# The context of cross-attention: turned by VectorE instead of TensorE, for all batches but the first

## The reference

```python
a = _layer_norm(audio_kv, ln_gamma, ln_beta)              # 16 x 375 x 512
Q = (hidden_states @ Wq.T).reshape(B, Tt, HEADS, HEAD_DIM).transpose(0, 2, 1, 3)
K = (a @ Wk.T).reshape(B, Ta, HEADS, HEAD_DIM).transpose(0, 2, 1, 3)
V = (a @ Wv.T).reshape(B, Ta, HEADS, HEAD_DIM).transpose(0, 2, 1, 3)
scores = jnp.einsum('bhtd,bhsd->bhts', Q, K) * scale       # 16 heads of 32
scores = jnp.where(mask, scores, jnp.float32(-jnp.inf))
attn = jax.nn.softmax(scores, axis=-1)
out = jnp.einsum('bhts,bhsd->bhtd', attn, V)
return hidden_states + jnp.tanh(gate) * (out @ Wo.T)
```

## Time and profile before

| | |
|---|---|
| median of 3 runs | 1399.43 us (1397.38 to 1405.21) |
| the profiled execution: its own time | 1399.84 us |
| the profiled execution: span, first to last instruction | 1398.0 us |
| mean granted TensorE clock over the span | 0.979 |
| TensorE busy | 1319.0 us (94% of the span) |
| VectorE, ScalarE, GpSimd busy | 939.5, 752.2, 528.5 us |

### The profile page before, as it was taken

How to read it: one execution, slowest core, us unless ns; L and a number is a source line. 1 busy time by engine, 2 the same in 40 slices (tenths; PEclk the granted TensorE clock), 3 DMA queues, 4 the chain that set the end, 5 groups by cost and what they waited for, 6 DMA issues and landing times.

```text
span 1398.0 us, 42906 instructions
## 1 busy us (share of the span) xinstructions
PE 1319.0 (94%) x17120; PEld 936.5 (67%) x17120; DVE 939.5 (67%) x2416; ACT 752.2 (54%) x1804; POOL 528.5 (38%) x582
## 2 busy tenths in 40 slices
PE   6999999999999999897899999999999999999967
PEld 5777777777777777666666666766676666667624
DVE  3555555555555555547578888888888789887852
ACT  4776677676676677532434453445444544454342
POOL 2221112222222222113547545654566355644550
PEclk9999999999999999987899999999999999999978
DMA  7333322222222222213000010010100010000000
GB/s 228 100 105 107 98 63 69 75 71 70 65 76 76 76 69 92 63 50 136 15 14 22 22 28 14 23 27 21 24 14 26 21 28 11 25 21 21 8 15 14
DMA packets 39402, 73.48 MB, mean 53 GB/s; under 512 B 17781, under 2 KB 20469, under 8 KB 37701
## 3 DMA queue, kind: packets, MB, share of 16 engines
q1 hardware_dynamic: 39237, 71.01, 17.2%
HBM read 60.01 MB, written 7.57 MB: 48 GB/s over the span
## 4 chain that ended last, share of the span: by engine, by line
PE 73%; DVE 13%; issue 8%; ACT 2%; DMA 2%; POOL 1%; SPq 1%; DVEq 0%; POOLq 0%; ACTq 0%
PE b_bank L2017 15%; PE b_bank L2023 12%; PE ring_bank L703 7%; PE ring_bank L704 6%; PE ring_bank L705 6%; PE av_bank L789 4%; PE score_banks L762 4%; DVE probs L450 3%; PE b_bank L2132 3%; PE score_banks L749 3%; PE b_bank L2158 2%; DVE bv L1404 2%; DVE probsT L467 2%; PE av_bank L775 2%; DVE ktil L1398 1%
## 5 line engine op out<-in xcount | busy, mean ns | idle before, releaser
L1139 POOL TENSOR_TENSOR rst<-rp,st 128x448 f32<-128x448 f32 x192 | 202.5, 1078 | 34.9 <-DVE st L1425 32.0
L450 DVE CUSTOM_DVE_ANT_0 probs<-score_banks,unmask 112x375 f32<-112x375 f32 x256 | 124.9, 545 | 93.0 <-issue 93.0
L595 ACT ACTIVATE probs<-probs,least_inv 112x375 f32<-112x375 f32 x256 | 152.7, 609 | 32.5 <-DVE least_inv L450 32.5
L467 DVE SCALAR_TENSOR_TENSOR probsT<-score_banks,least_cols 125x448 f32<-125x448 f32 x192 | 108.0, 618 | 54.2 <-PE score_banks L762 51.8
L610 ACT ACTIVATE probsT<-probsT,key_mask 125x448 f32<-125x448 f32 x192 | 114.7, 662 | 47.6 <-DVE probsT L467 47.4
L1131 POOL TENSOR_TENSOR xm<-mixed,xa 128x448 f32<-128x448 f32 x80 | 89.6, 1129 | 96.1 <-DVE mixed L1354 90.7
L375 POOL TENSOR_TENSOR ctx_rstd<-ctx_var_eps,a_eps_exp 125x3 f32<-125x3 f32 x16 | 13.9, 866 | 272.7 <-DVE ctx_var_eps L423 272.7
L340 POOL TENSOR_TENSOR aT_lo<-whole,aT_hi 128x375 fp32r<-128x375 f32 x64 | 59.0, 922 | 152.3 <-ACT whole L576 150.2
L703 PE MATMUL ring_bank<-aT_hi,wk_lo 128*128 128x376 f32 x256 | 91.2, 356 | 0.9 <-issue 0.9
L1159 POOL TENSOR_TENSOR cen_r<-wkv,sq_r 128x448 fp32r<-128x448 f32 x15 | 17.1, 1140 | 196.6 <-ACT sq_r L1829 196.6
L1354 DVE SCALAR_TENSOR_TENSOR mixed<-b_bank,vec_sb,sx 128x112 f32<-128x112 f32 x320 | 82.5, 324 | 5.6 <-POOL xm L1131 3.9
(11 more groups left out here) (197 smaller groups left out, 3156.6 us busy)
## 6 DMA issues: line engine op xcount, KB each, us to landing
least_cols<-values_of_two_batches SPq DMA_DIRECT2D x32, 437.5 KB
ctx_tok<-in_ctx SPq DMA_DIRECT2D x16, 672.0 KB
xT_sb<-in_xT SPq DMA_DIRECT2D x16, 224.0 KB, 3.0
inv_cols<-values_of_two_batches SPq DMA_DIRECT2D x128, 28.0 KB, 3.7
x_tok<-in_x SPq DMA_DIRECT2D x16, 224.0 KB, 2.7
x_between_layers<-x_tok SPq DMA_DIRECT2D x16, 224.0 KB, 4.6
b_x<-x_between_layers SPq DMA_DIRECT2D x16, 224.0 KB, 2.6
out_dram<-ln_tok SPq DMA_DIRECT2D x16, 224.0 KB, 2.3
```

The lines of the kernel that those rows point to most:

```text
L450: dve.tensor_tensor_reduce(out=probs[:, g % 2, i], in0=score_bank[0:T, i, 0:TC], in1=unmask[:, m[1]], scale=-SCALE, scalar=-LOWEST, op0=AL ...
L467: dve.scalar_tensor_tensor(out=probsT[:, g % 2, k].rearrange("p (i t) -> p i t", t=T), in0=score_bank[0:TK, :, k * T:(k + 1) * T], scalar= ...
L595: act.activation(probs[:, g % 2, i], probs[:, g % 2, i], ACT.Exp, scale=-1.0, bias=least_at(m, g, i), accum_out=sums[:, g, i:i + 1]).then_ ...
L1139: pool.tensor_tensor(by_chunk(rst[:, j % NPROD]), by_chunk(rp[:].rearrange("p c t -> p (c t)")), state_of(j), ALU.mult).then_inc(s_pprod, 1)
```

## The change

From batch 1 on TensorE no longer transposes the context. The context is loaded a second time in blocks of 32 tokens by 32 channels (`ctx_quads`: four quarters of the partitions hold four blocks of 128 channels), VectorE turns the blocks of 32 by 32 (`turn_ctx`, four instructions), GpSimd subtracts the means (`centre_ctx`), VectorE multiplies with the inverse deviations (`scale_ctx`), ScalarE applies gamma and beta in place (`affine_aT`) and rounds to `aT_hi` (`copy_aT`). Means and inverse deviations now lie along the free dimension, so they go to DRAM and come back on all 128 partitions (`spread_stats`). The first batch goes the old way. The channels are in another order over partitions, so `wk`, `wv`, gamma and beta are loaded in pieces; tokens are in plain order, so the two masks are read plainly (`key_mask8`). `least_cols` comes in two transfers, 112 and 13 partitions. Queries are projected in three calls, one of which stands where three of four turned chunks stood.

```diff
 
-RING = ["K0", "S1", "K1", "K2", "K3", "V0", "V1", "V2", "S0", "T0", "T1", "T2", "T3", "qa", "qb"]
-RING_START = ["T0", "T1", "T2", "T3", "qa", "qb"]
+RING = ["K0", "S1", "K1", "K2", "K3", "V0", "V1", "V2", "S0", "qa", "qb", "qc"]
+RING_START = ["T0", "T1", "T2", "T3", "qa", "qb", "qc"]
+QUERY = {"qa": (0, 1), "qb": (1, 2), "qc": (2, 4)}
 RING_FIRST = [u for u in RING if u != "S1"]
-RING_NEXT_LAST = [u for u in RING if u[0] not in "Tq"]
+RING_NEXT_LAST = [u for u in RING if u[0] != "q"]
...
+    def load_quads(sp, b):
+
+        if at_least(b, 2):
+            sp.wait_ge(s_turned, count(later(b, -2), 1, 1))
+        else:
+            sp.wait_ge(s_ring, unit_done((-1, 1), f"T{C - 1}"))
+        tokens = A["ctx"][index(b)]
+        for q in range(QUADS):
+            channels, rows = slice(q * P, (q + 1) * P), q * BLOCK
+            sp.dma_start(ctx_quads[rows:rows + BLOCK, 0:TB - 1],
+                             tokens[0:TC - TAIL, channels].rearrange("(k r) d -> r k d", r=BLOCK)).then_inc(s_quads, 16)
+            sp.dma_start(ctx_quads[rows:rows + TAIL, TB - 1], tokens[TC - TAIL:TC, channels]).then_inc(s_quads, 16)
...
+            if is_batch(b, 1):
+                sp.wait_ge(s_ctxn, 2)
+            elif at_least(b, 1):
+                sp.wait_ge(s_stats, count(later(b, -1), 2, 1))
...
+        def spread_stats(b):
+            sp.wait_ge(s_rstd, count(b, 1, 1))
+            sp.dma_start(stats_in_dram(b).rearrange("a (p k) -> p a k", k=KT), meanvar[:]).then_inc(s_stat_out, 16)
+            sp.wait_ge(s_stat_out, count(later(b, -1), 16, 16))
+            sp.dma_start(stat_rows[:], stats_in_dram(b).rearrange("(o a) t -> o a t", o=1).broadcast_to([P, 2, TC])).then_inc(s_stat_in, 16)
...
-            sp.dma_start(least_cols[:, 2 * half:2 * half + 2],
-                         rows_in_dram(half, 0).rearrange("(o g) f -> o g f", o=1).broadcast_to([TK, 2, HG * T])).then_inc(s_least_in[half], 16)
+            for part in CTX_PARTS:
+                sp.dma_start(least_cols[part, 2 * half:2 * half + 2],
+                             rows_in_dram(half, 0).rearrange("(o g) f -> o g f", o=1).broadcast_to(
+                                 [part.stop - part.start, 2, HG * T])).then_inc(s_least_in[half], 16)
...
+        def load_turned(name):
+            for q in range(QUADS):
+                sp.dma_start(W[name][q * BLOCK:(q + 1) * BLOCK], A[name][:, q].rearrange("(c j) d -> j c d", j=BLOCK)).then_inc(s_w[name], 16)
...
+        for q in range(QUADS):
+            for i, name in enumerate(("ln_gamma", "ln_beta")):
+                sp.dma_start(affine_ctx[q * BLOCK:(q + 1) * BLOCK, i], A["vec"][:, VEC[name], q].rearrange("(c j) -> j c", j=BLOCK),
+                             allow_slow_non_contiguous=True).then_inc(s_w["vec"], 16)
+        sp.wait_ge(s_ctx, 32)
         load_x((0, 0))
         sp.dma_start(wq[:], A["wq"]).then_inc(s_w["wq"], 16)
-        sp.dma_start(W["wk"][:], A["wk"]).then_inc(s_w["wk"], 16)
+        load_turned("wk")
         sp.dma_start(mask8[:], A["mask"].rearrange("(o b) t -> o b t", o=1).broadcast_to([T, B, TC])).then_inc(s_w["mask"], 16)
-        sp.dma_start(W["wv"][:], A["wv"]).then_inc(s_w["wv"], 16)
+        load_turned("wv")
         load_ctx((0, 1))
         load_x((0, 1))
         sp.dma_start(gate[:], A["gate"].broadcast_to([T, 1])).then_inc(s_w["gate"], 16)
-        sp.dma_start(key_mask8[:], A["mask"].rearrange("b (p k) -> p b k", p=TK),
+        sp.dma_start(key_mask8[:], A["mask"].rearrange("b (k p) -> p b k", p=TK),
                      allow_slow_non_contiguous=True).then_inc(s_w["key_mask"], 16)
-        sp.dma_start(wo[:], A["wo"]).then_inc(s_w["wo"], 16)
+        load_quads(sp, (0, 1))
...
             if normalise and not is_batch(n, B - 2):
                 load_x(later(n, 2))
+            if normalise:
+                spread_stats(later(n, 1))
+            if is_batch(n, 0):
+                sp.dma_start(wo[:], A["wo"]).then_inc(s_w["wo"], 16)
...
             if normalise and not is_batch(n, B - 2):
                 load_ctx(later(n, 2))
+                load_quads(sp, later(n, 2))
...
+        def centre_ctx(b):
+            pool.wait_ge(s_stat_in, count(later(b, -1), 16, 16))
+            pool.wait_ge(s_turned, count(later(b, -1), 1, 1))
+            for h in range(2):
+                part = ctxT[:, 2 * h:2 * h + 2, 0:TC]
+                pool.tensor_tensor(part, part, stat_rows[:, 0:1].broadcast_to([P, 2, TC]), ALU.subtract).then_inc(s_cent, 1)
...
+        def turn_ctx(b):
+            dve.wait_ge(s_quads, count(later(b, -1), 32 * QUADS, 32 * QUADS))
+            dve.wait_ge(s_split, count(later(b, -1), C, C))
+            for c in range(C):
+                last = dve.transpose(ctxT[:, c].rearrange("p (k r) -> p k r", r=BLOCK), ctx_quads[:, :, c * BLOCK:(c + 1) * BLOCK])
+            last.then_inc(s_turned, 1)
+
+        def scale_ctx(b):
+            for h in range(2):
+                dve.wait_ge(s_cent, count(later(b, -1), 2, h + 1))
+                part = ctxT[:, 2 * h:2 * h + 2, 0:TC]
+                dve.tensor_tensor(part, part, stat_rows[:, 1:2].broadcast_to([P, 2, TC]), ALU.mult).then_inc(s_ctxn, 1)
...
                 return last_step(m, l)
             if finish:
                 scale_attn(l, 1)
+            if normalise:
+                ln_stats(later(n, 1))
             if attend:
                 invert_sums(m, 1)
             if finish:
                 residual(l)
             if attend:
                 shift_scores(m, 0)
+            if normalise:
+                turn_ctx(later(n, 1))
...
             if project:
                 mask_scores(n, 0, range(HG))
             if is_batch(n, 0):
@@ -523,13 +601,11 @@
             if attend:
                 shift_scores(m, 1)
             if normalise:
-                ln_stats(later(n, 1))
+                scale_ctx(later(n, 1))
             if is_batch(n, B - 1):
                 second.stats1((0, 0))
             if project:
                 mask_scores(n, 1, range(HG))
-            if normalise:
-                ln_apply(later(n, 1))
             if is_batch(n, B - 1):
...
+        def affine_aT(b, c):
+            act.wait_ge(s_ctxn, count(b, 2, c // 2 + 1))
+            act.activation(ctxT[:, c, 0:TC], ctxT[:, c, 0:TC], ACT.Identity, scale=affine_ctx[:, 0, c:c + 1],
+                           bias=affine_ctx[:, 1, c:c + 1]).then_inc(s_whole, 1)
...
+            if normalise:
+                for c in range(C):
+                    affine_aT(p, c)
             if attend:
                 exps_key_major(m, 2)
             if project:
@@ -659,26 +748,28 @@
...
             if project:
                 copy_rows(n, 0)
             if normalise:
-                for c in range(3):
+                for c in range(C):
                     copy_aT(p, c)
+                copy_query(p, "a")
             if attend:
                 exps_key_major(m, 3)
             if is_batch(n, B - 1):
                 second.xa_affine((0, 0))
             if normalise:
-                copy_aT(p, 3)
-                copy_query(p, "a", slice(0, 2))
+                copy_query(p, "b")
             if project:
                 exps(n, 2, range(HG))
                 exps(n, 3, range(HG))
             if normalise:
-                copy_query(p, "b", slice(2, 4))
...
@@ -849,8 +943,7 @@
                 scores(n, 2)
                 turn_rows(n, 0)
             if normalise:
-                for c in range(3):
-                    transpose_ctx(p, c)
+                project_query(p, "a")
             if attend:
                 weigh_values(m, 2)
                 key_major_scores(m, 3)
@@ -858,20 +951,19 @@
                 pe.wait_ge(s_ringev, unit_done(n, "V2"))
                 second.transpose_x((0, 0))
             if normalise:
-                transpose_ctx(p, 3)
-                project_query(p, "a", (0, 1))
+                project_query(p, "b")
             if project:
                 scores(n, 3)
             if attend:
                 weigh_values(m, 3)
             if normalise:
-                project_query(p, "b", (2, 3))
-
-        pe.wait_ge(s_w["ident"], 16)
+                project_query(p, "c")
```

154 lines of the change are left out of this document (88 added, 66 removed).

## The result

| | before | changed |
|---|---|---|
| median | 1400.49 us, 4 runs (1397.38 to 1405.21) | 1413.26 us, 4 runs (1412.03 to 1418.06) |
| ratio, 95% interval | | 1.0103 (1.008 to 1.0126) |
| span of the profiled execution | 1398.0 us | 1410.2 us |

What follows compares the result with a forecast made beforehand. TensorE, busy 94%, was taken as full, with a second chain through VectorE and back behind it. 1399.8 + 12.1 + 1.8 + 0.7 - 2.3 - 1.5 - 1.4 = 1409.2 us, range 1395 to 1419.

Steps and rivals of the forecast that it cites:

- main term: Start, SyncE's queue: 6,000 mask runs delay `ctx_quads`, so VectorE's first maxima and V0 come late; +12.1 us, bounds +6.7 and +20.
- first maxima and V0 late: Start: first maxima at 38.1 us instead of 25.96, held by `ctx_quads` behind the mask, V0 moving with them; +12.1 us.
- the clock after the stand: Start: TensorE, after standing 12 us between K3 and V0, runs at half clock for a while; +1.8 us.
- `wv_lo` beside `centre_ctx`: Step 0: VectorE's and GpSimd's work come at the same time and slow four instructions; +0.7 us, between 0 and 1.4.
- transposes out, step 0: Step 0: `scores(0, 2)` to `scores(0, 3)` shrinks from 5.52 to 3.2 us; -2.3 us, bounds -2.3 and 0.
- transposes out, 14 steps: Steps 1 to 14: only the second chain link shortens, 3.00 to 2.89 us; 14 x 0.11 = -1.5 us, bounds 0 and -21.
- `least_cols` in two parts: Step 16: landing 1.5 us sooner removes VectorE's wait of 1.47 us; -1.4 us, bounds -1.5 and 0.
- The term of the steps: Step 5: TensorE waits 0.5 to 0.7 us before `key_major_scores(m, 3)`, about 1.2 before `scores(n, 3)`; step 0.1 us shorter.
- rival C: Start: it costs more, with mask runs at twice the price; 1417 us, 8%.
- Rival A: Steps: the 1.5 us of transposes come back in full each step, the chain having room; 1389.7 us, 12%.
- Zeros: Steps: VectorE's, GpSimd's and ScalarE's new work and SyncE's queue there cost 0 us.
- Rival D: Every step: `scale_ctx` waits for `centre_ctx` because the means land late; one us a step gives 1423 us, 10%.

Runs made afterwards that it cites:

- weights_whole: The changed kernel with `wk` and `wv` loaded in one transfer each, in runs of 8,192 bytes instead of 2,048; 1410.75 us, ratio 1.0083 to the kernel before.
- mask_bytes: The kernel before with `key_mask8` read in 6,000 runs of one byte instead of 2,000 of three; 1400.61 us, ratio 1.0005.
- fill: The changed kernel with `project_value(n, 2)`'s last chunk behind `scores(n, 2)` and query unit a behind `key_major_scores(m, 3)`; 1403.29 us, ratio 1.0028 to the kernel before.
- fill_before: The kernel before with only `project_value(n, 2)`'s last channel chunk moved behind `scores(n, 2)`; 1402.14 us, ratio 1.0024.
- least_parts: The kernel before with `least_cols` sent in two parts of 112 and 13 partitions, nothing else; 1398.13 us, ratio 0.9991.
- start_free: The changed kernel with `key_mask` sent behind `wo` and step 0's old VectorE and ScalarE order, except `ln_stats` ahead of the maxima; 1411.02 us, ratio 1.0078.
- mask_late: The changed kernel with `key_mask` sent behind `wo` in step 0 instead of ahead of `ctx_quads`; 1412.37 us, ratio 1.0102 to the kernel before.
- own_queue: The changed kernel with `key_mask` sent from ScalarE's queue and, in step 0, the kernel before's order on VectorE and ScalarE; 1410.7 us, ratio 1.0084.
- mask_act: The changed kernel with `key_mask` sent from ScalarE's queue, ahead of all ScalarE does, instead of SyncE's; 1413.32 us, ratio 1.0101 to the kernel before.
- two_parts: The changed kernel with 750 mask runs ahead, 5,250 from ScalarE's queue at step 0's end, and step 0's old VectorE and ScalarE order; 1410.37 us, ratio 1.0075.

## Why the prediction was right, point by point

I said 1409 us, 1395 to 1419, slower with 63%. It is 1413.26, by the mechanism that I had named. But the main term was too small by 9.4 us, two gains were larger than I had them (by 1.9 and 0.9 us), and one gain of 3.9 us was not foreseen.

| step of the sum | predicted | measured | shown by |
|---|---|---|---|
| first maxima and V0 late | +12.1 | +21.5 | timelines |
| the clock after the stand | +1.8 | +2.45 | V0 to the second `scores`: 5.42 less 2.97 |
| `wv_lo` beside `centre_ctx` | +0.7 | 0 | they did not meet: 2.49 us as before |
| transposes out, step 0 | -2.3 | -2.2 | 23.96 to 21.74 |
| transposes out, 14 steps | -1.5 | -2.4 | 21.70 to 19.27 |
| `least_cols` in two parts | -1.4 | -3.3 | 19.27 to 16.0 |
| start of the second layer | none | -3.9 | 16.0 to 12.1 |
| sum on 1399.84 | 1409.2 | 1412.0 | |

The measured terms are differences along one timeline, so that they add up shows nothing by itself. That 1413 lies in my forecast's own band of 1405 to 1414 is partly luck: with the losses of the first three rows as measured and all gains as I had them, the sum would have been 1418.6, at the upper edge of the range.

**The main term** failed in four places. I let the mask's runs begin at 23.2 us as before; they began at 27.1, 3.9 later, because `wk` and `wv` now come in pieces with runs of 2,048 bytes (weights_whole gives 3.8 of it back). I had missed that edit's price. The runs took 10.8 us instead of 8.1 (mask_bytes): between my middle and rival C's price, which was twice. SyncE was therefore free at 37.3, not 30.7, after an issue of 22.5 us where I had said 16. And `ctx_quads` landed 8.2 us after that, not 5.5: I had counted its issues and a latency, but not that its own 1,500 runs of 512 bytes follow one another for 7 us. Turning took 1.96 us against my 1.84.

**The term of the steps** was right in kind. Waits of 0.34 and 1.05 us stand where I had put 0.5 to 0.7 and 1.2, and the links are 3.06 and 2.90. Rival A (the transposes' time comes back) fell, and fill shows why: without the transposes the chain sets the time, and starting it 0.7 us sooner shortens each step by as much. fill_before agrees for the other side, with half of the edit: with the transposes TensorE is full and no order of this kind helps. What the removal freed is room, and the unchanged order of TensorE left it empty.

**Zeros.** VectorE's, GpSimd's and ScalarE's new work in the steps cost nothing, as said: a step is 0.17 us shorter, not longer. Rival D fell: `scale_ctx` waited for `centre_ctx` 5.2 us in all, in two places.

**Step 16** gave more than its wait of 1.47 us because behind the shorter stand the granted clock was 1.00 and not 0.50. The Trainium skill, DMA: Bandwidth & Descriptors, was of two minds; the traces (a wait of 0.82 us instead of 2.39, in least_parts too) agree with "Why a DMA increments its semaphore by 16 and not by 1", and not with "Rules for kernel authors", as far as that one wait goes.

**The second layer's gain** I can only read, not claim to have tested. The kernel before, then the changed kernel (SyncE and TensorE):

```profile
623.64 0.33 SPq L262 DMA_DIRECT2D x_between_layers<-x_tok  x1
627.08 0.35 SPq L1086 DMA_DIRECT2D b_wo<-in_b_wo  x1
...
645.29 3.99 PE L2158 MATMUL b_bank<-vbd,kz 64*32 64x128 f32 x128 [2.32 <-DMA vbd<-vtok]
```

```profile
639.66 0.33 SPq L299 DMA_DIRECT2D x_between_layers<-x_tok  x1
641.92 0.35 SPq L1178 DMA_DIRECT2D b_wo<-in_b_wo  x1
...
658.89 3.21 PE L2250 MATMUL b_bank<-vbd,kz 64*32 64x128 f32 x128
```

The store takes 3.44 us until SyncE goes on, and 2.26 in the changed kernel; behind it stand the weights, and behind them `vbd`. Of the 3.9 us the wait for `vbd` is 2.3, and 0.8 is that the 128 matmuls behind it take 3.21 us instead of 3.99; the rest comes by 680 us and I did not trace it. In the kernel before three packets of the two queues of instructions, one of 16 KB and two of 8 KB, fall into the store (its transfers from 623.6 to 627.1 us, by queue: packets, MB, share of the engines):

```profile
q8 instruction: 1, 0.02, 2.6%
q14 instruction: 2, 0.02, 1.2%
```

In the changed kernel none does; the packet of 16 KB comes 4.8 us behind the store's issue. This holds in every trace: 0.6 to 0.7 us behind the issue, with one or two of 8 KB, in the four kernels with transposes, and 3.2 us or more in the ten without. All three kernels that I made from the one before take 3.3 to 3.5 us there and wait 1.9 to 2.7 us for `vbd`; all nine made from the changed one take 2.3 and wait at most 0.3. So this part belongs to the program, not to chance. That it is these packets, or which of them, was not tried by itself.

## What to carry to other kernels

Count runs, not bytes: a table of 6 KB in 6,000 runs cost 7 to 8 us more than in 2,000, the largest single part of what the start lost, and wherever I put it, it delayed something that was soon needed. If work is taken off a full engine and its time doesn't come back, look for the chain that now shows as short waits, and move other work into them; in the steps the removal alone was worth 2.4 us, half of the reordering alone nothing, removal and reordering together 12. Putting the wait for a first load behind what the next engine already waits for brought V0 forward by 5 and 8 us (start_free against mask_late, own_queue against mask_act) but the time by no more than 3, since the next link took over: the whole path, the rows of the load itself included, has to be added up.

## What the hardware showed that I had not expected

Two engines at once. GpSimd's passes of 750 elements took 1.80 us, and VectorE's `scale_ctx` of the same size 0.93 us, but 2.51 once:

```profile
L506 DVE TENSOR_TENSOR ctxT<-ctxT,ctx_stat_rows x30: 926/932/2507, 54.7 to 555.0; 128x750 f32<-128x750 f32 x30
```

The long one began at 54.73 us, while GpSimd's second pass ran until 56.44; the 1.58 us over are nearly that overlap of 1.71. In start_free `wv_lo` came beside GpSimd's mask work and took 4.01 us instead of 2.49. The Trainium skill, SBUF — State Buffer, "Who interferes with whom", has the two exclude each other for a whole instruction; these rows agree, and my +0.7 for such a meeting would have been too low by half (4.01 less 2.49 is 1.5).

The price of a run. On SyncE's queue 6,000 runs took 10.8 to 11.9 us in the six kernels that have them there in one piece, while the DMA engines show a share of 0.56. The Trainium skill, DMA: Bandwidth & Descriptors, "Why a DMA increments its semaphore by 16 and not by 1", gives a transfer whose slowest dimension is 125 five engines of the sixteen. The row does not bear that out by itself: five engines busy without a break are a share of 0.31. By that rule parts of 112 and 13 partitions would shorten the mask, as least_parts shortened the wait for `least_cols`; no run here shows it. The same page, "Queues, rings and completion order", has each engine take turns between queues; mask_act and two_parts agree: beside the runs of ScalarE's queue the first keys were 6.9 us late, and the write of the means, which took SyncE 2.1 us in step 5 of the changed kernel, took 11.0 in two_parts.
